# Linear attention beside a routed FFN: small matrix products dealt out among the large ones, bulk transfers moved, state products on the whole TensorE array

## What is computed

```python
xn = layernorm(x)                               # no gain or bias
# retention: linear attention with a decay mask, 16 heads of 16
q, k, v = (split_heads(xn @ W + b) for W, b in ((Wq, bq), (Wk, bk), (Wv, bv)))
mask = where(i >= j, 0.95 ** (i - j), 0)
out = (einsum('bhid,bhjd->bhij', q, k) * mask) @ v      # no softmax
y = groupnorm(out @ Wo + bo, groups=16, over=(channels of the group, S)) * gamma + beta
# FFN with 8 experts; each takes its best 128 of the 512 tokens of a batch
probs = softmax(xn @ gate_w)
top_p, top_idx = top_k(transpose(probs), 128)
z = scatter_add(top_idx, (gelu(xn[top_idx] @ w1) @ w2) * top_p)
return x + y + z
```

## Time and profile before

| | |
|---|---|
| median of 3 runs | 2489.22 us (2487.41 to 2489.69) |
| profiled execution | 2482.65 us |
| its span, first to last instruction | 2480.8 us |
| mean granted TensorE clock | 0.975 |
| TensorE matmul busy | 2323.8 us, 94% |
| VectorE busy | 1305.8 us, 53% |
| ScalarE busy | 990.0 us, 40% |
| GpSimd busy | 1277.9 us, 52% |
| code fetched, queue q8 | 194 packets, 3.18 MB |

### The profile page before, as it was taken

The page is one execution under the profiler, slowest core; times in us unless marked ns, Lnnn a source line. Parts: engine busy times, 40 slices in busy tenths (PEclk is TensorE's granted clock), DMA queues, the critical chain, the costliest instruction groups (busy, mean ns, idle before and its releaser), DMA issues.

```text
span 2480.8 us, 76765 instructions
## 1 busy us (share of the span) xinstructions
PE 2323.8 (94%) x31948; PEld 2024.0 (82%) x31948; DVE 1305.8 (53%) x2531; ACT 990.0 (40%) x1801; POOL 1277.9 (52%) x2088
## 2 busy tenths in 40 slices
PE   6999999889999995899999999999999999999997
PEld 5777777777777773789999999999999999999996
DVE  2455545466655556764455445545544554555443
ACT  4555555555545552333333333333333333333332
POOL 4334344433343342556666666666666666665453
PEclk9999999999999997899999999999999999999998
DMA  3122222222222211322332323323223323223222
GB/s 121 54 85 73 71 71 74 85 71 78 72 79 71 71 54 50 91 43 47 78 51 44 80 47 63 65 44 82 42 49 78 49 44 81 47 47 47 45 49 26
DMA packets 129262, 156.22 MB, mean 63 GB/s; under 512 B 11008, under 2 KB 118656, under 8 KB 129024
## 3 DMA queue, kind: packets, MB, share of 16 engines
q0 software_dynamic: 49152, 67.14, 16.7%
q1 hardware_dynamic: 79872, 85.54, 10.8%
HBM read 85.53 MB, written 67.11 MB: 62 GB/s over the span
## 4 chain that ended last, share of the span: by engine, by line
PE 58%; POOL 1%; DVE 1%; issue 0%; DMA 0%; ACT 0%; POOLq 0%; DVEq 0%; ACTq 0%
PE hidden L1295 28%; PE y L1310 27%; PE xt L1282 2%; POOL out L1148 0%; POOL xg L1138 0%; DMA out<-y,scatter_idx 0%; DVE best_index L204 0%; DVE g_hi L1262 0%; DVE best L200 0%; DMA xg<-xn_rows,step_idx 0%; DVE g_lo L1264 0%; DVE rows L208 0%; DVE xt_lo L1251 0%; ACT y L1197 0%; ACT g L1211 0%
## 5 line engine op out<-in xcount | busy, mean ns | idle before, releaser
L1148 POOL DMA_INDIRECT out<-y,scatter_idx x256 | 430.7, 1683 | 412.1 <-ACT y L1197 352.6
L1262 DVE CAST g_hi<-g 128x512 fp32r<-128x512 f32 x512 | 289.7, 566 | 667.6 <-ACT g L1211 665.2
L1310 PE MATMUL y<-w_hi,g_hi 128*128 128x256 f32 x2048 | 571.3, 279 | 0.3 <-ACT y L1197 0.3
L1310 PE MATMUL y<-w_lo,g_hi 128*128 128x256 f32 x2048 | 565.8, 276 | 0.0
L1310 PE MATMUL y<-w_hi,g_lo 128*128 128x256 f32 x2048 | 565.6, 276 | 0.0
L1211 ACT ACTIVATE g<-hidden 128x512 f32<-128x512 f32 x512 | 306.8, 599 | 402.9 <-PE hidden L1295 402.9
L1295 PE MATMUL hidden<-xt_hi,w_lo 128*128 128x512 f32 x1024 | 404.5, 395 | 0.0
L1295 PE MATMUL hidden<-xt_lo,w_hi 128*128 128x512 f32 x1024 | 402.7, 393 | 0.0
L1295 PE MATMUL hidden<-xt_hi,w_hi 128*128 128x512 f32 x1024 | 399.5, 390 | 1.5 <-DVE xt_lo L1251 1.5
L1264 DVE TENSOR_TENSOR g_lo<-g,g_hi 128x512 fp32r<-128x512 f32 x512 | 386.2, 754 | 17.6
L1310 PEld LDWEIGHTS y<-w_hi,g_hi 128*128 128x128 f32 x2048 | 384.6, 188 | 0.5 <-ACT y L1197 0.5
(11 more groups left out here) (150 smaller groups left out, 3615.1 us busy)
## 6 DMA issues: line engine op xcount, KB each, us to landing
x<-in_x SPq DMA_DIRECT2D x32, 512.0 KB, 5.6
w_stage<-in_w SPq DMA_DIRECT2D x16, 1024.0 KB, 6.1
xn_rows<-xn SPq DMA_DIRECT2D x32, 512.0 KB, 3.7
res<-in_x SPq DMA_DIRECT2D x32, 512.0 KB, 4.0
out<-res SPq DMA_DIRECT2D x32, 512.0 KB, 2.9
xg<-xn_rows,step_idx POOLq DMA_INDIRECT x256
out<-y,scatter_idx POOLq DMA_INDIRECT x256, 3.9
cst<-in_cst SPq DMA_DIRECT2D x1, 436.0 KB, 4.2
```

What stands on the lines that cost most here:

```text
L1148: pool.indirect_dma_start(out_rows, bass.IndirectOffsetOnAxis(sidx[:, k:k + 1], 0), y[:, k, :], None, compute_op=ALU.add).then_inc(scatter ...
L1262: dve.tensor_copy(g_hi[:, m, :], g32[m % 4][:]).then_inc(gh_ready, 1)
L1310: last = pe.matmul(yb[k % 2][:, 0:D], g_[:, m, cols], w[par][:, m, :], start=i == 0, stop=i == 3 * FT - 1)
```

## The change

- **Order on TensorE.** `scores` is now called per chunk, `values` per chunk and half (of 32 records). The first half's `scores` follow `query_key` 1; `query_key` 2 and 3 come after them. `inter` stands between `value_gate` 0 and 1. The eight parts of `values` lie between `value_gate`, `turn_keys` and `turn_x`; only the last two stand together, right ahead of the running state. Both `turn_y` come before the own chunk, which is now last.
- **State products.** `tm` has 128 columns in place of 32 (zeros outside the heads' own blocks), so that one 128x128 product takes the place of four of 32x32: 14 instructions, 28 records a batch.
- **VectorE.** `states` writes 14 x 128 columns (each of the 14 x 32 in PSUM read four times). Softmax stands ahead of `states`; `masked` 0 and 1 stand together ahead of the group moments.
- **GpSimd.** `decayed` ahead of `gates`.
- **SyncE.** The store of `xn` and the load of `x` go out in the next pass, after `query_key` 0; `out` and `res` after `query_key` 2.

```diff
@@ -49,7 +49,7 @@
 C_ID, C_MASK, C_G, C_BD, C_QD, C_PAR, C_KD, C_OFF, C_N = \
-    0, 128, 192, 320, 352, 864, 866, 870, 872
+    0, 128, 192, 320, 448, 960, 962, 966, 968
 V_BQ, V_BK, V_BO, V_GA, V_BE, V_N = 0, 2, 4, 6, 8, 10
@@ -274,7 +274,7 @@
         vm = [sb(f"v_parity{i}", [P, TT, VW]) for i in range(2)]
-        tm = [sb(f"state{i}", [P, NSUB - 1, DH, 2 * HD]) for i in range(2)]
+        tm = [sb(f"state{i}", [P, NSUB - 1, DH, P]) for i in range(2)]
         s_sb = [sb(f"s_sb{i}", [P, PAIRS, 512]) for i in range(2)]
@@ -339,7 +339,7 @@
         gones = cst[:, C_G:C_G + P]
-        bdm = cst[:, C_BD:C_BD + 2 * HD]
+        bdm = cst[:, C_BD:C_BD + P]
         qdec = cst[:, C_QD:C_QD + S]
@@ -383,6 +383,17 @@
             def one(b, par):
+                f, l = b + 1, b + 1
+                if has(f):
+                    sp.wait_ge(qk_mm, 4 * f + 1)
+                if has(l):
+                    sp.wait_ge(xn_ready, TT * l + TT)
+                    sp.dma_start(xn_v[l], xn[:]).then_inc(xn_stored, 16)
+                    if has(l + 2):
+                        sp.dma_start(xb[1 - par][:], x_v[l + 2]).then_inc(x_in[1 - par], 16)
+                if has(f):
+                    sp.wait_ge(qk_mm, 4 * f + 3)
                 if has(b - 2):
@@ -391,12 +402,6 @@
                     sp.dma_start(res[:], x_v[b - 1]).then_inc(res_in, 16)
-                if has(b + 2):
-                    sp.wait_ge(xn_ready, TT * b + 3 * TT)
-                    sp.dma_start(xn_v[b + 2], xn[:]).then_inc(xn_stored, 16)
-                    if has(b + 4):
-                        sp.dma_start(xb[par][:], x_v[b + 4]).then_inc(x_in[par], 16)
             passes(one)
@@ -477,9 +482,9 @@
                     biased(f, fp, 3)
-                    gates(f)
                     for h in range(DH):
                         decayed(f, fp, h)
+                    gates(f)
             def first(b, par):
@@ -661,9 +666,11 @@
                 n = (NSUB - 1) * DH
-                dve.tensor_tensor(tm[fp][:].rearrange("p j h x -> p (j h) x"),
-                                  sbk[:, 0, 0:n * 2 * HD].rearrange("p (g x) -> p g x", x=2 * HD),
-                                  bdm.unsqueeze(1).broadcast_to([P, n, 2 * HD]), ALU.mult).then_inc(tm_ready, 1)
+                dve.tensor_tensor(tm[fp][:].rearrange("p j h (r x) -> p (j h) r x", r=PAIRS),
+                                  sbk[:, 0, 0:n * 32].rearrange("p (g x) -> p g x", x=32).unsqueeze(2)
+                                  .broadcast_to([P, n, PAIRS, 32]),
+                                  bdm.rearrange("p (r x) -> p r x", r=PAIRS).unsqueeze(1)
+                                  .broadcast_to([P, n, PAIRS, 32]), ALU.mult).then_inc(tm_ready, 1)
             def group_moments(a, h):
@@ -713,12 +720,12 @@
                     softmax(b, par)
-                for h in range(DH):
-                    if has(b):
-                        masked(b, h)
-                    if has(a):
+                if has(b):
+                    masked(b, 0)
+                    masked(b, 1)
+                if has(a):
+                    for h in range(DH):
                         group_moments(a, h)
-                if has(a):
                     group_averages(a)
@@ -738,11 +745,10 @@
                         residual(a, j)
-                if has(f):
-                    states(f, fp)
                 if b not in (MID, B):
                     softmax(b, par)
+                if has(f):
+                    states(f, fp)
                 if b == B:
@@ -834,29 +840,30 @@
                 last.then_inc(kt_ready, 1)
-            def scores(b, par, z):
-                if z == 0:
+            def scores(b, par, c):
+                z = c // 2
+                if c == 0:
                     pe.wait_ge(s_ready, 4 * b)
...
                     pe.wait_ge(qm_ready, 2 * b + 2)
-                else:
+                elif c == 2:
                     if has(b - 1):
...
                     pe.wait_ge(s_ready, 4 * b + 2)
-                for c in (2 * z, 2 * z + 1):
-                    for h in range(DH):
-                        for s in range(2):
-                            toks = slice(c * P + s * SUB, c * P + (s + 1) * SUB)
-                            for p in range(PAIRS):
-                                rows = slice(32 * p, 32 * p + 32)
-                                at = (c - 2 * z) * 256 + h * P
-                                last = pe.matmul(sbk[s * SUB:(s + 1) * SUB, p, at:at + P], k32[par][rows, h, toks],
-                                                 qm[par][rows, h, :, toks], start=True, stop=True)
-                last.then_inc(s_mm, 1)
+                for h in range(DH):
+                    for s in range(2):
+                        toks = slice(c * P + s * SUB, c * P + (s + 1) * SUB)
+                        for p in range(PAIRS):
+                            rows = slice(32 * p, 32 * p + 32)
+                            at = (c - 2 * z) * 256 + h * P
+                            last = pe.matmul(sbk[s * SUB:(s + 1) * SUB, p, at:at + P], k32[par][rows, h, toks],
+                                             qm[par][rows, h, :, toks], start=True, stop=True)
+                if c % 2:
+                    last.then_inc(s_mm, 1)
             def inter(b, par, z):
@@ -869,30 +876,28 @@
                         at = h * 256 + c * SUB
-                        for p in range(PAIRS):
-                            rows = slice(32 * p, 32 * p + 32)
-                            pe.matmul(ob[rows, s, at:at + SUB], tm[par][rows, g - 1, h, :],
-                                      qd[par][rows, h, g * SUB:(g + 1) * SUB], start=g in (1, 2) and h == 0,
-                                      stop=False, skip_group_check=True)
-            def values(b, par, c):
+                        pe.matmul(ob[:, s, at:at + SUB], tm[par][:, g - 1, h, :],
+                                  qd[par][:, h, g * SUB:(g + 1) * SUB], start=g in (1, 2) and h == 0, stop=False,
+                                  skip_group_check=True)
+            def values(b, par, c, h):
                 z = c // 2
...
                 pe.wait_ge(s_ready, 4 * b + 2 * z + 2)
-                for h in range(DH):
-                    for a in range(2):
-                        for s in range(2):
-                            rows = slice(s * SUB, (s + 1) * SUB)
-                            for p in range(PAIRS):
-                                out_rows = slice(32 * p, 32 * p + 32)
-                                at = h * 256 + c * SUB
-                                src = (c - 2 * z) * 256 + h * P + a * SUB
-                                col = a * D + h * P + 32 * p
-                                last = pe.matmul(ob[out_rows, s, at:at + SUB], vm[par][rows, c, col:col + 32],
-                                                 s_sb[z][rows, p, src:src + SUB], start=False, stop=a == 1,
-                                                 skip_group_check=True)
-                last.then_inc(av_done, 1)
+                for a in range(2):
+                    for s in range(2):
+                        rows = slice(s * SUB, (s + 1) * SUB)
+                        for p in range(PAIRS):
+                            out_rows = slice(32 * p, 32 * p + 32)
+                            at = h * 256 + c * SUB
+                            src = (c - 2 * z) * 256 + h * P + a * SUB
+                            col = a * D + h * P + 32 * p
+                            last = pe.matmul(ob[out_rows, s, at:at + SUB], vm[par][rows, c, col:col + 32],
+                                             s_sb[z][rows, p, src:src + SUB], start=False, stop=a == 1,
+                                             skip_group_check=True)
+                if h:
+                    last.then_inc(av_done, 1)
             def running_state(b, f, fp, own_half):
@@ -961,10 +966,11 @@
                     query_key(b, f, 1)
-                    query_key(b, f, 2)
                 if has(b):
                     scores(b, par, 0)
-                if has(f):
+                    scores(b, par, 1)
+                if has(f):
+                    query_key(b, f, 2)
                     query_key(b, f, 3)
@@ -973,6 +979,9 @@
                     value_gate(b, f, 0)
+                if has(b):
+                    inter(b, par, 1)
+                if has(f):
                     value_gate(b, f, 1)
@@ -983,36 +992,42 @@
                     route.turn_rows(pe, 0 if b == MID else 1, sbk[:, 2, :])
+                if has(b):
+                    values(b, par, 0, 0)
                 if has(f):
...
                 if has(b):
-                    scores(b, par, 1)
+                    scores(b, par, 2)
+                    scores(b, par, 3)
+                    values(b, par, 0, 1)
                 if has(f):
...
                 if has(b):
-                    inter(b, par, 1)
+                    values(b, par, 1, 0)
                 if has(f):
...
                 if has(b):
```

(24 more changed lines are left out.)

## The result

The change takes 2468.23 us at the median of 20 runs (2463.33 to 2488.57); the kernel before, run beside it on the same chips, 2487.99 us (20 runs). The ratio is 0.9937, with a 95% interval of 0.992 to 0.9954: faster, by 20 us at the medians, where 4 us slower was forecast. The medians alone would give 0.9921; the ratio is that of the means, and three of the change's 20 runs took 2486 to 2489 us. Measured again later it was 2468.42 against 2488.07, ratio 0.9918 (0.9904 to 0.9932).

The account below looks back on a forecast made before the run. TensorE was taken to set the first stage's pass length, with stalls for code; 25.35 + 1.4 + 0.8 - 0.2 + 1.5 + 0.5 = 29.35 us against 29.13, giving 2487 in profile, 2493 us at the median, range 2455 to 2528.

Parts of the forecast that it names:

- work alone, dealt out, group sums: First-stage pass: 25.35 us without stalls, +0.8 for switches between small tiles and whole array, -0.2 for later group sums.
- wait for `tm_ready`: TensorE's `scores` waits 1.5 us a pass for the wider state copy (2.0 us), queued behind softmax on VectorE.
- fetch stalls: TensorE waits for code blocks at small products: 0.5 us a pass left of 3.8 with all they bring.
- half clock: TensorE's granted clock at 0.50, 1.2 in place of 2.4 GHz, after long stalls; no such spells forecast after the change.
- the state products themselves: On TensorE, 28 whole-array records at 0.12 us, 3.4, plus 0.15 for returns, replace 2.1 us: net +1.4 a pass.
- The carry from profile to median: Changes were added to the profiled 2482.65 us, then 6.6 us added to reach the median of runs.
- Code as what TensorE waits for: TensorE's "issue" stalls are waits for code in blocks of some 256 instructions, slower to come while 512 KB transfers run.
- Rival 4: Code isn't what TensorE waits for, so nothing is won: 29.13 + 3.5 us a pass, 2595 us; chance 0.02.
- Dealing out costs +0.8 a pass: TensorE's switches between small tiles and whole array: groups go from 7 to 9, +0.8 us a pass, bounds +0.3 and +1.3.
- rival 1: VectorE isn't late with the state copy, so `scores` doesn't wait: -1.3 us a pass, 2448 us; chance 0.28.
- Rival 2: Whole-array state products load and stream in series, 0.17 us a record: +1.4 us a pass more, 2535 us; chance 0.2.
- Rival 3: TensorE's stand of 1.5 us lowers its clock, 3 us at half speed, some 1 us a pass: 2523 us; chance 0.07.

Follow-up runs that it names:

- e2: The changed kernel with the narrow state again (`tm` of 32 columns, 448-element copy, four small products per wide one); 2405.74 us, ratio 0.9653.
- e1: The changed kernel with softmax behind `states` again, as in the kernel before, nothing else changed; 2420.17 us, ratio 0.971.
- e8: The changed kernel with both the narrow state and softmax behind `states`; 2397.05 us, ratio 0.9672.
- e3: The kernel before with SyncE's new order of transfers alone; 2425.11 us, ratio 0.9724.
- e7: The kernel before with 32 more transposes (64 instructions) at TensorE's very start, shifting its code; 2509.5 us in one run.
- e10: e8 run again: the changed kernel with narrow state and softmax behind `states`; 2398.88 us, ratio 0.9634.
- e5: The kernel before with TensorE's new order and the order of `masked` alone; narrow state, old transfers, old place of softmax; 2449.78 us, ratio 0.9852.
- e6: The kernel before with the wide state alone (128-column `tm`, its copy and products), copy ahead of softmax; 2475.54 us, ratio 0.9968.
- e4: The changed kernel with SyncE's old order of transfers; 2513.79 us, ratio 1.0107.

## Why the prediction was off

The sum was wrong in its sign by terms that nearly cancel. Taken apart in the traces: e2, whose pass has the new order with the old state, has 25.83 us of work a pass (26.77 less 0.94 idle, over its passes at full clock); e1, with the wide one, 26.68 (27.15 less 0.47).

| term, us a pass | forecast | measured | from |
|---|---|---|---|
| work alone, dealt out, group sums | 25.35 + 0.8 - 0.2 = 25.95 | 25.83 | e2 |
| state products | +1.4 | +0.85 | e1 less e2 |
| wait for `tm_ready` | +1.5 | +1.42 | idle, the change less e1 |
| fetch stalls | +0.5 | +0.47 | idle of e1 |
| half clock | 0 | +0.37, +0.12 | 20.5 and 6.8 us, half of it taken as lost |
| sum | 29.35 | 28.94, 28.69 | passes of 28.94 and 28.77 |

- **The step that failed: "the state products themselves".** Their net cost was put at +1.4 us a pass and is +0.85, 0.55 less, some 16 us over 30 passes; that decides the sign. For the new ones 28 x 0.12 = 3.4 and 0.15 for the returns was forecast, 3.55. The timeline has 2.96 up to the next dense product, and the first dense product behind each of the two groups takes 0.085 longer: 3.13 in all, which is 28 x 0.112 with the ends already in it. So 0.22 of the miss is the price of a record, 0.112 and not 0.12, and the 0.15 for the returns was not needed on top. The rest is rounding and the old ones, put at 2.1, which come to about 2.2. In e8, start to start, they take 1.83, and the dense products next to their two groups are dearer: the one ahead takes 0.32 and 0.215 us where it takes 0.23 and 0.12 ahead of the wide ones (e1), and the one behind 0.23 in place of 0.12. Dense products and transposes together take 15.85 us a pass with the 32x32 groups and 15.6 with the wide ones. I took a value between the two loads of the earlier trace rows, 0.11 each, and the transposes of the earlier trace rows, 0.13. But that 0.13 is the mean of a group of eight with its ends: from record to record they go at 0.109, the first takes 0.166 and the last 0.203. Both rows had the same pace, and it was the right one. The Trainium skill (TensorE: Matmul & The Clock Gate, LDWEIGHTS) has columns / 1.2 ns, 107 ns for 128: the runs show 112, closer to it than to my 120, and I set it aside as roughly the same.
- **The carry from profile to median.** I added 6.6 us, since the profile of before lay so far under its median. That of the change lay 6.8 us above its own (2474.99 against 2468.23), with 20.5 us at half clock; its second profiled execution, with 6.8 us, took 2468.34. So the 25 us between 2493 and 2468 are 12 us of passes (0.41 x 30) and 13 us of this carry. Against the second execution they are 19 and 6.
- **Code as what TensorE waits for** held. e3 shortens the stalls without touching TensorE's work, e7 moves them by moving the code. Rival 4 is out.
- **Dealing out costs +0.8 a pass**: too much. From e3 to e2 the work of passes at full clock goes from 25.85 to 25.83 us, and to 25.80 and 25.83 in e8 and e10: nothing. The base hid this: "25.35" for the work alone took off 0.22 for each stall and was 0.5 too low against those 25.85, so that the two errors nearly cancel in the first line of the table. That this line came out right is luck.
- **The wait behind the softmax** held: the copy takes 2018 ns (2.0), the wait is 1.39 us a pass (1.5), and rival 1, no wait, is out. Removing it in e1 gives 48 us: that is the price of two calls in exchanged order, and without it the change would have been worth 68 to 70 us.
- **Rival 2**, 0.17 us a record, is refuted by 0.112. **Rival 3**, a clock lowered by the stand of 1.5 us, does happen, but seldom: I had no half-clock time in the sum, and five of the six spells of the change's profiled execution, and both of the second one's, begin within 2 us of the end of such a wait, all of 1.68 to 1.80 us. But 22 of the first execution's 27 waits from 100 to 930 us leave the clock at 1.00. So it costs 0.1 to 0.3 us a pass, counted as in the table, and not 1. e1, with no such wait, has none. One of the five, and the granted clock behind it (the 0.50):

```profile
208.79 1.20 PE L863 MATMUL scores<-q_parity,k 32*64 32x128 f32 x64 [1.80 <-DVE state L669]
...
210.50:212.50 2.00, 2.00 (x7) 1.52 (x6) 1.97 (x8) 0.00 (x0) 0.72 (x4) 0.50 0.00 0
```

- **Where the gain went.** Moving the transfers alone brings 65 us (e3). The new order on TensorE, with `masked` and `decayed` moved, brings 24 more (e3 to e10, both with `states` ahead of the softmax): 89 in all. With the old transfers it had brought 36 (e5). What `masked` and `decayed` give by themselves was not run. The wide state then takes back 18 to 23 (e8 and e10 to e1; 0.61 to 0.77 us a pass), since its gain of 10 us in e6 came with 0.70 us less idle time a pass, of which the other two parts leave little (0.52 in e8). The softmax ahead takes 48 with a copy of 2.0 us (e1 to the change), where with one of 0.6 it takes 6. The net is 20. Some of the parts can hold a share of what e7 shows, since they change where TensorE's code blocks end: dealing out and the wide state (e2, e5, e6, e8, e10). The 65, the 48, the 46 of e4 and the 6 can't: in those pairs TensorE runs the same code.

## What to carry to other kernels

Where the idle time of TensorE is "issue" in the middle of many tiny products, look at what the DMA queues do in those microseconds: moving bulk transfers beside long products was worth more here than any change to the products. Two changes that remove the same stall don't add up, and a step made three times longer has to be read together with what was put ahead of it on its engine. When a sum's terms nearly cancel, the price taken from a row decides the sign: take the pace from the middle of a group, from one record to the next, and look for the cost of its ends in the neighbours too. Don't carry one profiled execution's distance to its median over to another kernel.

## What the runs showed of the hardware

- Reading 448 PSUM elements a partition four times over by broadcast costs what the other two sizes say of 1792: 614, 1216 and 2018 ns for 448, 1024 and 1792 elements, about 1.05 ns each and 0.15 us.
- A plain float32 product with 128x128 weights and 64 columns is issued every 0.112 us (the change), as its weight loads are; transposes with 128 columns go at 0.109 (before). The columns don't show in either. Going from dense products to 32x32 tiles costs 0.09 us in the dense product ahead and 0.11 in the one behind (e8); with 128x128 float32 in their place nothing ahead and 0.085 behind (e1).
- 64 instructions ahead of everything moved the stalls of a kernel from 2.65 to 2.91 us a pass, its half-clock time from 59.3 to 108.0 us and its time by 24 us (one run). Where code blocks end is a hidden variable in any comparison of such kernels. I had not expected it to be as large as the change measured here, and e6's 10 us is no more than that.
- The same program had 20.5 us at half clock in one profiled execution and 6.8 in another, with the same idle time of 1.89 us a pass. The two times are 6.7 us apart (2474.99 and 2468.34), the 28 passes 4.9 (810.30 and 805.44): a third to a half of the 13.7 us. In the spell above the dense products follow one another after 0.43 us in place of 0.23.
- The expert stage, whose code the change leaves alone, takes 1479 to 1480 us from its first dense product on in twelve of the thirteen profiles, and 1497.5 in e10's, where its dense products start 0.232 us apart at the median in place of 0.229. TensorE is at half clock for 21 to 25 us of it in the twelve and for 22 in e10's, so the granted clock is not the difference; the cause is open.
